# Scale steps, three row buffers, a new order of steps, and the last residual added by VectorE in a two-layer transformer kernel

## The reference

```python
def fp4_quant_dequant(x):
    xb = x.reshape(shape[:-1] + (shape[-1] // 16, 16))
    scale = jnp.maximum(jnp.max(jnp.abs(xb), axis=-1, keepdims=True) / 6.0, 1e-12)
    xn = xb / scale
    q = _GRID[jnp.searchsorted(_MID, jnp.abs(xn))] * jnp.sign(xn) * scale
...
# layer 0: linear attention with two decays per head (a scan), residual, layer norm
# layer 1: RWKV time mixing and channel mixing (a scan), residual
# each layer: x = x + gate_a * mixer(norm(x)); x = x + gate_b * ffn(norm(x)),
#   ffn(h) = fp4_linear(silu(fp4_linear(h, w_gate)) * fp4_linear(h, w_up), w_down), inner width 352
```

## Time and profile before

| | |
|---|---|
| median of 3 runs | 1400.71 us |
| the profiled execution's own time | 1395.93 us |
| its span, first to last instruction | 1394.0 us |
| TensorE matmul busy | 1228.5 us (88%) |
| VectorE busy | 1121.0 us (80%) |
| ScalarE busy | 1062.6 us (76%) |
| GpSimd busy | 222.7 us (16%) |
| mean granted TensorE clock | 0.957 of full |

### The profile page before, as it was taken

The page is one execution under the profiler, slowest core; times in us unless marked ns, Lnnn a source line. Parts: engine busy times, 40 slices in busy tenths (PEclk is TensorE's granted clock), DMA queues, the critical chain, the costliest instruction groups (busy, mean ns, idle before and its releaser), DMA issues.

```text
span 1394.0 us, 18809 instructions
## 1 busy us (share of the span) xinstructions
PE 1228.5 (88%) x5710; PEld 732.2 (53%) x5710; DVE 1121.0 (80%) x1619; ACT 1062.6 (76%) x2849; POOL 222.7 (16%) x286
## 2 busy tenths in 40 slices
PE   5677888989899999989898999989898999979787
PEld 2234364655656564646556564746455555647453
DVE  5848587988989798979889897979798897965424
ACT  5163868889797979798797979797897979786653
POOL 1000202121211103021212111030212112110100
PEclk9888999999999999999999999999999999989899
DMA  4000000000000000000000000000000000000000
GB/s 133 0 0 8 1 1 8 1 16 1 16 1 16 1 15 2 1 16 1 16 1 16 1 16 1 9 8 1 16 1 16 1 16 1 9 1 8 0 8 8
DMA packets 21488, 13.67 MB, mean 10 GB/s; under 512 B 1552, under 2 KB 20624, under 8 KB 21392
## 3 DMA queue, kind: packets, MB, share of 16 engines
q1 hardware_dynamic: 12944, 8.29, 2.0%
q10 hardware_dynamic: 8448, 4.20, 1.0%
HBM read 8.28 MB, written 4.19 MB: 9 GB/s over the span
## 4 chain that ended last, share of the span: by engine, by line
PE 67%; ACT 12%; DVE 11%; issue 6%; POOL 3%; SPq 0%; DMA 0%; ACTq 0%; DVEq 0%; POOLq 0%
PE ps L1105 10%; PE ps L1218 6%; PE ps L1317 4%; PE ps L923 4%; PE ps L1310 4%; PE ps L1184 3%; PE ps L1017 3%; PE ps L1256 3%; PE ps L1013 3%; PE ps L903 3%; PE ps L1257 3%; ACT hq L502 2%; PE ps L977 2%; PE ps L937 2%; POOL rstd_of_a L411 2%
## 5 line engine op out<-in xcount | busy, mean ns | idle before, releaser
L1105 PE MATMUL ps<-wguT,hqcol 128*128 128x352 f32 x512 | 168.2, 470 | 20.4 <-ACT hqcol L676 12.5
L1569 DVE TENSOR_TENSOR_SCAN state<-beta,outer 128x512 f32<-128x512 f32 x128 | 149.2, 1206 | 0.0
L1105 PEld LDWEIGHTS ps<-wguT,hqcol 128*128 128x128 f32 x512 | 93.1, 191 | 78.2 <-issue 24.6
L418 POOL TENSOR_TENSOR var_of_f<-squares_f,eps_sum 128x4 f32<-128x4 f32 x32 | 12.1, 378 | 656.3 <-ACT hq L502 656.3
L1419 DVE SCALAR_TENSOR_TENSOR hid<-hidcol,hid 128x1408 f32<-128x1408 f32 (+1 forms) x68 | 106.2, 1566 | 6.0 <-ACT hidcol L693 5.9
L1218 PE MATMUL ps<-hidcol,wdT 128*128 128x256 f32 (+1 forms) x384 | 92.5, 384 | 0.4 <-ACT hidcol L702 0.4
L1641 DVE TENSOR_TENSOR hid<-th,ps 128x352 f32<-128x352 f32 x128 | 63.3, 512 | 25.2 <-ACT th L684 16.2
L977 PE MATMUL ps<-state,const 128*32 128x512 f32 x256 | 70.9, 831 | 8.8 <-DVE state L1595 8.4
L1595 DVE TENSOR_TENSOR state<-state,qshare 128x1024 f32<-128x1024 f32 x64 | 76.8, 1221 | 2.2
L903 PE MATMUL ps<-const,hq 128*128 128x128 f32 x128 | 34.8, 335 | 48.7 <-ACT hq L492 47.4
L700 ACT ACTIVATE hidcol<-ps 128x512 f32<-128x512 f32 x64 | 38.1, 595 | 51.6 <-PE ps L1184 51.6
(11 more groups left out here) (236 smaller groups left out, 3291.4 us busy)
## 6 DMA issues: line engine op xcount, KB each, us to landing
xa<-in_x SPq DMA_DIRECT2D x16, 256.0 KB, 2.8
out<-xb ACTq DMA_DIRECT2D x16, 256.0 KB, 2.2
const<-in_const SPq DMA_DIRECT2D x1, 848.0 KB, 6.5
state<-in_wmod SPq DMA_DIRECT2D x1, 768.0 KB, 4.5
outer<-in_wqk SPq DMA_DIRECT2D x1, 256.0 KB, 4.5
ex<-in_w_gate_up SPq DMA_DIRECT2D x2, 128.0 KB, 2.6
fw_key<-in_fw_key SPq DMA_DIRECT2D x1, 256.0 KB, 3.0
fw_val<-in_fw_val SPq DMA_DIRECT2D x1, 256.0 KB, 3.8
```

Of the source, the lines that this page charges most:

```text
L1105: t_.matmul(bank(f"f{l}_{'gu'[g]}{t}")[:, 0:I_FF], hqcol[l][:, t * P:(t + 1) * P], wguT[:, l, g, :], start=True, stop=True).then_inc(s_gu[ ...
L1569: return v.tensor_tensor_scan(state[:, m, c, :], beta[:, m, :], src, 0.0, ALU.mult, ALU.add)
```

## The change

`scale_blocks` no longer makes `back`: the multiplication carries the minus sign instead, and `round_blocks` multiplies by `scale`. `xa` and `xb` get a third buffer each. The store moves to SyncE's queue, ahead of the load of the same turn. The last residual is no longer added by TensorE: `b6r_1` only turns `gcol` to rows (four transposes), and a new VectorE step `add_rows` adds them from PSUM to `xb` in place; the copy on ScalarE goes. The order lists of TensorE, VectorE, ScalarE and GpSimd, the bank table and the waits of `freed` that follow from it are new. The lists also begin at another place of the turn (at `c6` on TensorE); as `do` leaves out pairs that don't exist, this moves no instruction by itself.

```diff
-        xa = sb("xa", [P, 2 * NT, H])
-        xb = sb("xb", [P, 2 * NT, H])
+        xa = sb("xa", [P, 3 * NT, H])
+        xb = sb("xb", [P, 3 * NT, H])
...
@@ SyncE
             def load_x(i):
-                before_last(sp, s_x2mm, i)
+                if i >= 3:
+                    sp.wait_ge(s_x2mm, i - 2)
...
+            def store(j):
+                sp.wait_ge(s_x4, j + 1)
+                sp.dma_start(out_v[j, :, :, :], of_pair(xb, j)).then_inc(s_out[j % 3], 16)
+
             def body(n):
+                do(store, n - 4)
                 do(load_x, n)
...
@@ ScalarE
             def b6c(l, i):
-                if l == 0:
-                    act.wait_ge(s_x2mm, i + 1)
...
-                else:
-                    act.wait_ge(s_x4mm, i + 1)
-                    s.activation(of_pair(xb, i), bank("f1_x").rearrange("p (t h) -> p t h", h=H), ACT.Copy).then_inc(s_x4, 1)
+                act.wait_ge(s_x2mm, i + 1)
+                if i >= 3:
+                    act.wait_ge(s_out[i % 3], 16 * (i // 3))
+                rows_out("a1", i, "f0_x", of_pair(xb, i), s_x2)
...
@@ TensorE
             def b6r_1(j):
                 after(pe, s_gd[1], j, SEQ)
-                freed(pe, s_cch, j + 1)
-                freed_at_ends(pe, s_th[1], j, NT, 3)
-                rows_of(bank("f1_x"), of_pair(xb, j))
-                add_columns(bank("f1_x"), gcol[1]).then_inc(s_x4mm, 1)
+                freed(pe, s_hqc[1], j, 2, 2)
+                for t in range(NT):
+                    last = t_.transpose(bank("f1_x")[:, t * P:(t + 1) * P], gcol[1][:, t * P:(t + 1) * P], ident)
+                last.then_inc(s_x4mm, 1)
...
             def body(n):
-                do(a3b, n - 1, 1)
                 do(a2, n - 1, 0)
...
+                do(a3, n, 1)
+                do(a3b, n, 1)
+                do(c5, n - 2)
...
@@ VectorE
-            def scale_blocks(part, src, dst, scales, at, nb, put_back, floor):
+            def scale_blocks(part, src, dst, scales, at, nb):
...
                 if part == 1:
-                    v.tensor_scalar(back, top, -put_back, -SCALE_MIN, ALU.mult, ALU.min)
-                    return v.tensor_scalar(scale, top, 1 / 6.0, floor, ALU.mult, ALU.max)
+                    return v.tensor_scalar(scale, top, 1 / 6.0, SCALE_MIN, ALU.mult, ALU.max)
                 if part == 2:
                     return v.reciprocal(inv, scale)
-                return v.scalar_tensor_tensor(dst, src, TIE_DOWN, spread(inv, nb), ALU.mult, ALU.mult)
+                return v.scalar_tensor_tensor(dst, src, -TIE_DOWN, spread(inv, nb), ALU.mult, ALU.mult)
...
-                return v.tensor_tensor(dst, dst, spread(scales[:, 3, at:at + nb], nb), ALU.mult)
+                return v.tensor_tensor(dst, dst, spread(scales[:, 1, at:at + nb], nb), ALU.mult)
...
+            def add_rows(j):
+                dve.wait_ge(s_x3, j + 1)
+                dve.wait_ge(s_x4mm, j + 1)
+                v.tensor_tensor(of_pair(xb, j), of_pair(xb, j), bank("f1_x").rearrange("p (t h) -> p t h", h=H), ALU.add)\
+                    .then_inc(s_x4, 1)
...
                 do(a4, n - 1, 0, 0)
+                do(add_rows, n - 4)
                 at_start(late_weights, n - 1)
                 do(a5, n - 1, 0)
-                do(a4, n - 1, 0, 1)
                 do(a5, n - 1, 1)
                 do(mean_f1, n - 3)
+                do(a4, n - 1, 0, 1)
...
+                do(layer(b1m, 0), n - 1, 0)
+                do(c4t, n - 2)
+                do(layer(b1m, 0), n - 1, 1)
```

More of the change, by code:

```diff
@@ L227, in build @@
         hq = [sb(f"hq{l}", [P, NT, H]) for l in range(2)]
[L228 to L229 removed]
+        xblk = [sb(f"xblk{l}", [P, 3, NT * H // BLK]) for l in range(2)]
+        blk = [sb(f"blk{l}", [P, 3, NT * I_FF // BLK]) for l in range(2)]
         hqcol = [sb(f"hqcol{l}", [P, TOK]) for l in range(2)]
@@ L273, in build @@
         s_set_dve, s_set_act, s_set_pe, s_set_pool = sem("setup_dve"), sem("setup_act"), sem("setup_pe"), sem("setup_pool")
-        s_x = [sem(f"x_loaded{p}") for p in range(2)]
-        s_out = [sem(f"out_stored{p}") for p in range(2)]
+        s_x = [sem(f"x_loaded{p}") for p in range(3)]
+        s_out = [sem(f"out_stored{p}") for p in range(3)]
         s_lnc = sem("chain_ln_a0")
@@ L843, in body @@
                 do(c1n, n - 2)
-                do(a1n, n)
                 do(c1, n - 2, 0)
                 do(c1, n - 2, 1)
+                do(a1n, n)
+                do(c2s, n - 2)
                 do(a1, n, 0)
-                do(c2s, n - 2)
                 do(a5y, n - 1)
@@ L982, in a5 @@
                 if q == 0:
+                    freed(pe, s_hqc[0], i - 1, 2, 1)
+                    freed_at_ends(pe, s_outer, i, 2, 2)
+                else:
                     freed(pe, s_gd[0], i - 1, SEQ)
-                    freed_at_ends(pe, s_shch, i, 2, 1)
-                    run_idle(bank(f"a_s{q}"), i, {0: 8})
-                else:
-                    freed(pe, s_bm_th, i, 3, 3)
+                    freed_at_ends(pe, s_phi, i, 2, 1)
+                run_idle(bank(f"a_s{q}"), i, {0: 8 - 8 * q})
                 pe.wait_ge(s_share, i + 1)
@@ L1382, in body @@
                 do(b3_1, n - 3, 0)
+                do(a8, n - 1)
                 do(c3, n - 2, 1)
-                do(a8, n - 1)
+                do(a2, n, 0)
+                do(b3_1, n - 3, 1)
+                do(c3, n - 2, 2)
+                do(a3, n, 0)
+                do(b3_1, n - 3, 2)
+                do(b3_1, n - 3, 3)
+                do(b1T_0, n - 1)
+                do(a2, n, 1)
+                do(b1R_0, n - 1)
+                do(a3, n, 1)
+                do(a3b, n, 1)
+                do(c5, n - 2)
+                do(c7x, n - 2)
+                do(layer(b2, 0), n - 1)
+                do(b3_0, n - 1, 0)
+                do(b3_0, n - 1, 1)
+                do(c5n, n - 2)
+                do(b3_0, n - 1, 2)
+                do(b3_0, n - 1, 3)
+                do(c6r, n - 2)
             turns(pe, body)
@@ L1399, in spread @@
                 return t.unsqueeze(2).to_broadcast([P, nb, BLK])
-            def scale_blocks(part, src, dst, scales, at, nb, put_back, floor):
-                top, scale, inv, back = (scales[:, k, at:at + nb] for k in range(4))
+            def scale_blocks(part, src, dst, scales, at, nb):
+                top, scale, inv = (scales[:, k, at:at + nb] for k in range(3))
                 if part == 0:
```

553 lines of the change are left out of this document (262 added, 291 removed), and 10 rows, old and new, of the table BANK.

## The result

The changed kernel is slower: 1421.02 us (median; 1409.93 to 1421.8) against 1400.74 us, a ratio of 1.0126 with an interval of 1.0076 to 1.0176. The forecast was 1373 us, with a range up to 1390. The profiled execution took 1421.8 us (span 1420.0), 25.9 us more than that of before. The forecast for a turn was 75.2. One of the four executions of the changed kernel took 1409.93 us, at a mean granted clock of 0.947 against 0.938 in the others.

What follows compares the result with a forecast made beforehand. No engine alone was taken as the bound, but a loop of three legs through a turn. -1.65 us over 14 turns (-23.1), tail -3.9 and ramp -1 made -28: 1373 us from 1400.71, range 1355 to 1390.

Steps and rivals of the forecast that it cites:

- Leg 3: From the mean of the rows between the layers to `a6`: forecast -1.1 us a turn, bounds 0 and -1.2.
- `a4`'s last sum starts 1.1 us earlier: On TensorE: with `c1r` ahead of `a1`, `a4`'s last sum starts 1.1 us earlier, `a5y` and `a6` with it.
- its growth as a sign of being wrong: The prediction would be wrong if the piece of a turn at TensorE's lower clock grew; no size given.
- Leg 1: From `a6` to the end of `b1R_0`, TensorE's own work: `a3b` leaves it, -0.65 us a turn, bounds 0 and -0.86.
- Leg 2: From `b1R_0` to the mean between the layers: VectorE ends it, 0.1 us later a turn, bounds -0.9 and +1.0.
- Residual: `b6r_1`: 1.30 us a turn off TensorE's path; the addition puts 0.65 us on VectorE, bounds 0.58 and 0.69.
- scale steps: On VectorE: four instructions a turn go, 0.10 us each; three lie in its stretch of leg 2, -0.3 us.
- buffers: The row buffers: the store's buffer is next written a turn later with three buffers, so nothing gained or lost.
- store: On SyncE: the load waits for the addition and the store, but stays covered by 5 us or more; nothing.
- The tail's -3.9: Behind the last full turn, three residuals on the chain at 1.30 us each: -3.9 us.
- VectorE becomes the bound: Rival, `b1R_0` to the mean: VectorE gets 0.95 us more, a turn is 77.9 us, 1410 us in all; chance 0.07.
- clock: Rival: `b6r_1`'s transposes bring the 1.2 GHz level up to the first sums, up to 8 us a turn, 1490 us; chance 0.01.

Runs made afterwards that it cites:

- e1: The changed kernel with three idle TensorE products of 512 columns (the fill) ahead of `b1T_1` in every turn, so that the clock stays up: 1390.72 us, ratio 0.9933.
- e13: e10 with the change's new order of leg 3 added, on both TensorE and ScalarE: 1374.09 us, ratio 0.9841.
- e2: The kernel before with the same three idle products ahead of `b1T_1` in every turn: 1398.43 us, ratio 0.9986.
- e3: The kernel before with the new last residual alone (four transposes, addition on VectorE, no ScalarE copy), no idle products: 1390.88 us, ratio 0.9932.
- e4: The changed kernel with the old last residual put back (identity product on TensorE, copy on ScalarE), no idle products: 1416.4 us, ratio 1.0112.
- e7: The changed kernel with one idle product ahead of `b1T_1` in every turn, in place of three: 1403.38 us, ratio 1.0005.
- e12: The changed kernel with only `add_rows` moved behind the mean of the rows between the layers, no idle products: 1400.05 us, ratio 1.0003.
- e10: The kernel before with three idle products ahead of `b1T_1`, the new residual and the new scale steps, old order: 1384.37 us, ratio 0.989.
- e5: e1 with `add_rows` moved behind the mean of the rows between the layers: 1384.05 us, ratio 0.9875.
- e17: e13 with the change's three row buffers and the store on the load queue: 1373.87 us, ratio 0.9812.

## Why the prediction was wrong

Three legs were forecast at -0.65, +0.1 and -1.1 us; they came out at -0.05, +0.29 and +1.42. With the clock held (e1) the changed kernel takes 1390.72 us: of the 48 us between forecast and result the clock makes 30, the mis-sized terms the rest.

**Leg 3, the step that failed.** "`a4`'s last sum starts 1.1 us earlier" was costed with the clock of before. The order alone is worth -0.79 (e13, and e1 against e2); the missing 0.3 is `a1` on TensorE: in e1 it ends 0.3 us behind the last state (685.58 against 685.28), paced by ScalarE's rows. Then the clock takes 2.19. I saw the low clock there and that a turn with a longer slow piece takes 77.47 us, and named its growth as a sign of being wrong, but gave it 0.01 and placed it behind `b6r_1`; I never asked what the piece I had seen would cost once its cover was gone. Before, `a1n` stood ahead of `c1`'s columns on ScalarE, and a late `c1` held up only `c1r`. The timeline of TensorE in one of the turns of before that had a slow piece of 6.8:

```profile
831.97 1.54 PE L903 MATMUL ps<-const,hq 128*128 128x128 f32 x4 [2.76 <-ACT hq L492]
833.44 1.94 PE L977 MATMUL ps<-state,const 128*32 128x512 f32 x8
835.31 1.12 PE L1040 MATMUL ps<-const,hqcol 128*128 128x128 f32 x4
...
842.94 0.46 PE L1001 MATMUL ps<-const,hcolb 128*128 128x128 f32 x2 [0.79 <-issue]
```

From the start of `b1T_1` to `a6` it takes 10.97 us there, and in the new order 11.77 (613.11 to 624.88). Over all middle turns of the kernels that differ in little else, leg 3 goes by the slow piece of its turn like this:

| slow piece | old order (before, e2, e3) | new order (after, e1, e4, e7, e12) |
|---|---|---|
| none | 12.81 to 12.83, 13 turns | 11.99 to 12.05, 19 turns |
| 3.4 us | 12.81 to 12.83, 14 turns | 12.92 to 13.41, 16 turns |
| 6.8 us | 12.88 to 13.43, 9 turns | 14.03 to 14.48, 25 turns |

The new order is 0.8 us better with no slow piece and some 1 us worse with one of 6.8; a piece of 3.4, which the old order covers whole, already takes the gain. The reason is that the new order makes one chain of `c1`, `hcol`, `a1n`, `a1` and the last `a4`. That reason is argued from the rows; that the clock takes 2.1 us is shown.

**A step costed at nothing.** Moving `b1R_1` between the first two `a4` splits a pair. Apart, each takes 1.92 us at a clock of 0.50; before, both together took 1.94 (833.44). The groups of TensorE by line, for e10, e13, and the changed kernel:

```profile
L976 PE MATMUL ps<-state,const 128*32 128x512 f32 x256 | 55.8, 626 | 18.5 <-DVE state L1594 18.4
```

```profile
L976 PE MATMUL ps<-state,const 128*32 128x512 f32 x256 | 69.1, 626 | 7.4 <-DVE state L1594 7.1
```

```profile
L982 PE MATMUL ps<-state,const 128*32 128x512 f32 x256 | 95.3, 846 | 7.3 <-DVE state L1597 7.3
```

The same 256 products with the same mean cover 13.3 us more once they are apart, 0.83 a turn, which e13 pays out of idle time (18.5 to 7.4) and the changed kernel, at the lower clock, ahead of `c1`. By these rows `c1` could come some 1.9 us earlier there with the pair kept, an estimate (ScalarE has its rows by 617.30); that wasn't run.

**Leg 1.** -0.65 came out as -0.05. The 0.86 us of `a3b` went, but `b3_1` now waits 0.56 us for its bank (632.92 above: `f1_u0` shares bank 0 with `a_zT`, which ScalarE reads), and `b1T_0`, whose rows ScalarE writes just in time either way, takes 0.83 instead of 0.61. I had read the order list and not the bank table, which the change rewrites. That the two explain it is argued from the rows; no run gives `f1_u0` another bank.

**Leg 2.** +0.1 came out as +0.29, with the parts off in both directions: `c6b` 0.48 late instead of 0.9; then -0.19. TensorE waited 0.78 for `share` behind the addition, which I had costed on VectorE alone; VectorE had 0.49 us to spare at the mean and was not the end of this leg. e5 shows it. Against e17, with the same residual, the new order and banks of legs 1 and 2 cost 0.60 before `c6b` and 0.29 behind it.

**Residual, scale steps, buffers, store.** The residual, -1.30 on TensorE's path and +0.65 on VectorE's, was -0.48 a turn, the scale steps' -0.3 was -0.15, and the nothing of the buffers and the store was nothing (e17). Their sum with the order of leg 3 is -1.4 us a turn: e17 takes 1373.87 us, where the forecast for the whole change was 1373. That is a coincidence of totals (its turn is 75.45, and it has the fill). The tail's -3.9 didn't come: behind the fifteenth start, where it was forecast, the residual alone (e3) takes 119.8 us against 119.9, and the changed kernel 122.2. The first turn's 3.1 more is 1.2 of clock (81.94 against 80.69 in e1); the other 1.8 come with the new order of legs 1 and 2 (77.89 in e13), and no run takes them apart.

**Rivals.** None gave this. "VectorE becomes the bound" had the total nearest (1410) with the wrong engine; "clock" had the engine and the wrong place and size.

e13 and e17, both some 1374 us, are the shortest kernels of this study; they differ by less than their runs do.
